# Source indices of a graph kernel loaded once and copied into the gather slots by VectorE, in place of one DMA per tile

## The reference

```python
h = relu(layernorm(x));  z = h @ W                       # layer 1: attention, 8 heads of 16
e = leaky_relu(el[src] + er[dst]);  a = exp(e - max)     # el, er: z times attn_l, attn_r per head
x = x + segment_sum(z[src] * a, dst) / segment_sum(a, dst) + bias
h = relu(layernorm(x));  s, v = h @ W_up                 # layer 2: messages
w = silu(silu(edge_f @ A1 + b1) @ A2 + b2) @ A3
x = x + segment_sum(products of s[src], v[src], edge_y and w, dst) / 10 @ W_out
```

## Time and profile before

| | |
|---|---|
| median of 3 runs | 4219.83 us (4218.35 to 4221.5) |
| profiled execution: span, first to last instruction | 5708.3 us |
| busy in it: TensorE matmul / weight load | 3872.9 / 2962.4 us |
| busy in it: GpSimd / VectorE / ScalarE | 3121.2 / 1850.8 / 547.9 us |
| DMA | 239.77 MB, 42 GB/s on average |

### The profile page before, as it was taken

One profiled execution on the slowest core, in us unless ns is written; L12 is line 12 of the kernel. 1 busy time (PEld: TensorE's weight loads), 2 busy tenths in 40 slices (PEclk: granted clock), 3 DMA queues, 4 the chain that ended last, 5 costly groups with the idle time before them and its releaser, 6 DMA issues.

```text
span 5708.3 us, 68375 instructions
## 1 busy us (share of the span) xinstructions
PE 3872.9 (68%) x18070; PEld 2962.4 (52%) x18071; DVE 1850.8 (32%) x4774; ACT 547.9 (10%) x1093; POOL 3121.2 (55%) x3153
## 2 busy tenths in 40 slices
PE   3566666766666666666657776776777776667767
PEld 2455555555555555555545555555555555555545
DVE  6122222222222222222234443433333434333334
ACT  1000000000000000000021111111111111111111
POOL 4555555555555555555535555555555555555554
PEclk8555555555555555555567777777777877777777
DMA  3111111111111111111111111111111111111111
GB/s 75 40 40 40 40 40 41 41 42 40 41 40 41 40 41 39 41 40 40 40 43 41 42 45 41 44 45 41 42 43 43 44 44 41 44 40 43 42 41 34
DMA packets 259081, 239.77 MB, mean 42 GB/s; under 512 B 179890, under 2 KB 205596, under 8 KB 259068
## 3 DMA queue, kind: packets, MB, share of 16 engines
q0 software_dynamic: 100352, 212.14, 15.2%
q1 hardware_dynamic: 158572, 26.68, 2.6%
q10 hardware_dynamic: 144, 0.80, 0.0%
HBM read 229.11 MB, written 10.23 MB: 42 GB/s over the span
## 4 chain that ended last, share of the span: by engine, by line
another core or an unknown queue 43%; PE 22%; issue 17%; DVE 11%; DVEq 4%; ACT 2%; DMA 0%; ACTq 0%; SPq 0%
PE pair L1085 5%; PE pair L1050 5%; DVE share L809 4%; PE pair L1044 3%; PE pair L1083 3%; PE pair L1040 2%; DVEq L768 2%; ACT share L502 1%; PE pair L1062 1%; PE pair L1004 1%; PE pair L987 1%; DVE share L743 1%; DVE share L800 1%; DVE share L799 1%
## 5 line engine op out<-in xcount | busy, mean ns | idle before, releaser
L401 POOL DMA_INDIRECT rows<-z_tab,idx x1568 | 1531.6, 977 | 1290.3 <-DVEq L813 748.9
L401 POOL DMA_INDIRECT rows<-up_tab,idx x1568 | 1549.4, 988 | 1208.6 <-DVEq L896 718.1
L1004 PE MATMUL pair<-share 128*128 128x48 f32 x3136 | 1000.7, 416 | 122.6 <-issue 122.3
L1004 PEld LDWEIGHTS pair<-share 128*128 128x128 f32 x3136 | 808.4, 317 | 279.4 <-issue 273.3
L1085 PE MATMUL pair<-share 128*128 128x144 f32 x3136 | 859.4, 359 | 129.8 <-issue 129.3
L1083 PEld LDWEIGHTS pair<-share 128*128 128x128 f32 x3136 | 587.2, 219 | 443.2 <-issue 342.9
L1050 PE MATMUL pair<-a_bd,share 128*128 128x256 f32 x1576 | 465.9, 448 | 394.1 <-ACT share L504 371.1
L877 DVE TENSOR_TENSOR share<-share,y_sb 128x768 f32<-128x768 f32 x392 | 375.6, 958 | 977.1 <-remote 662.1
L1083 PE MATMUL pair<-share 128*128 128x48 f32 x3136 | 585.7, 269 | 140.0 <-issue 121.2
L1085 PEld LDWEIGHTS pair<-share 128*128 128x128 f32 x3136 | 561.3, 221 | 128.6 <-issue 128.0
L987 PE MATMUL pair<-er_win,share 96*128 96x32 f32 x1576 | 377.2, 404 | 333.0 <-issue 268.4
(11 more groups left out here) (138 smaller groups left out, 2085.3 us busy)
## 6 DMA issues: line engine op xcount, KB each, us to landing
rows<-z_tab,idx POOLq DMA_INDIRECT x1568
rows<-up_tab,idx POOLq DMA_INDIRECT x1568
idx<-in_src SPq DMA_DIRECT2D x396, 4.0 KB
er_win<-er_tab SPq DMA_DIRECT2D x396, 3.0 KB
ef_sb<-in_edge_f SPq DMA_DIRECT2D x198, 32.0 KB
z_tab<-rows SPq DMA_DIRECT2D x7, 476.0 KB, 3.1
y_sb<-in_edge_y SPq DMA_DIRECT2D x198, 16.0 KB
x_sb<-in_x SPq DMA_DIRECT2D x7, 448.0 KB, 6.9
```

What stands on the lines that cost most here:

```text
L401: pool.indirect_dma_start(out=rows[:, s, t, 0:width], out_offset=None, in_=table, in_offset=bass.IndirectOffsetOnAxis(ap=indices[:, t:t + ...
L1004: t.matmul(bank[2 + h][:, 0:WIN], msg[:, h, i, :], hot[:, s, i, :], start=(i == 0), stop=(i == T - 1))
```

## The change

A tile idx_all holds the source indices of all 200 tiles (196 and the first four again). One DMA on ScalarE's queue fills it at the start; for that the array is laid out with the partition first. Each loop's index DMA on SP, its semaphores and the `landed` count are gone. VectorE instead copies 128x8 indices from idx_all into the gathers' slot, at the place where the slot's old indices are known to be used: after L804 in the attention stage, and behind the wait for the rows in the message stage. Four such copies fill the slots before the first gather, ahead of L709. GpSimd waits for the count of copies, `idx_set`.

```diff
+        idx_all = sb("idx_all", [P, NG + U, T], I32)
...
-            for s in range(U):
-                sp.dma_start(idx[:, s, :], src[s, :, :]).then_inc(s_idx[s], 16)
             store_rows(s_in, ZW, z_tab)
-
-            def load_idx(s, group):
-                sp.dma_start(idx[:, s, :], src[bass.ds(group, 1), :, :].rearrange("a p t -> (a p) t"))\
-                  .then_inc(s_idx[s], 16)
...
                     load((s + AHEAD) % U, q * U + (s + AHEAD))
-                    hold(sp, s_l["landed"], i + 1)
-                    load_idx(s, q * U + (s + U))
...
-                            hold(pool, s_idx[s], (n + before) * 16 + 16)
+                            hold(pool, idx_set, (n + before) * U + (s + 1))
                             hold(pool, s_l["rows_free"], n * U + (s + 1))
...
             act.dma_start(dst_i, dst).then_inc(loads["dst"], 16)
+            act.dma_start(idx_all[:, :, :], src).then_inc(loads["src"], 16)
...
+            dve.wait_ge(loads["src"], 16)
+
+            def set_idx(s, group):
+                v.tensor_copy(idx[:, s, :], idx_all[:, bass.ds(group, 1), :].rearrange("p a t -> p (a t)"))\
+                    .then_inc(idx_set, 1)
+
+            for s in range(U):
+                set_idx(s, s)
...
                         dve.wait_ge(s_l1["rows"][s], q * (16 * T) + 16 * T)
-                        dve.sem_inc(s_l1["landed"], 1)
...
                         v.tensor_scalar(e3[3], e3[2], 0.0, None, ALU.min).then_inc(s_l1["score"], 1)
+                        set_idx(s, q * U + (s + U))
                         one_hot((s + 1) % U, q * U + (s + 1))
...
                                 dve.wait_ge(s_l2["rows"][s], q * (16 * T) + 16 * T)
-                                dve.sem_inc(s_l2["landed"], 1)
+                                set_idx(s, q * U + (s + U))
```

More of the change, by code:

```diff
@@ L177, in gnn_kernel @@
         loads = {n: sem(f"load_{n}") for n in
-                 ("x0", "x1", "const", "dst", "w", "attn", "bias", "mlp", "up", "out_w", "win")}
+                 ("x0", "x1", "const", "dst", "src", "w", "attn", "bias", "mlp", "up", "out_w", "win")}
         zeroed = sem("zeroed")
@@ L197, in edge_sems @@
         def edge_sems(tag, names):
-            return named(tag, ("rows_free", "added", "open", "landed") + names) \
+            return named(tag, ("rows_free", "added", "open") + names) \
                 | {n: sems(f"{tag}_{n}_slot", U) for n in ("rows", "in")}
-        s_idx = sems("idx", U)
+        idx_set = sem("idx_set")
         s_l1 = edge_sems("l1", ("hot", "turned", "hot_turned", "er", "score", "exp", "msg", "agg"))
@@ L312, in _ @@
                     sp.wait_ge(s_max["free"], g + 1)
-                    sp.dma_start(idx_max[:, :], src[bass.ds(g, 1), :, :].rearrange("a p t -> (a p) t"))\
-                      .then_inc(s_max["idx"], 16)
                     sp.dma_start(dst_row.rearrange("a (t p) -> a t p", t=T),
@@ L414, in _ @@
                 with pool.Fori(0, NG) as g:
-                    hold(pool, s_max["idx"], (g + 1) * 16)
+                    hold(pool, s_max["idx"], g + 1)
                     gather(0, idx_max, z_tab, ZW, s_max["rows"])
@@ L685, in _ @@
                 with dve.Fori(0, NG) as g:
+                    v.tensor_copy(idx_max[:, :], idx_all[:, bass.ds(g, 1), :].rearrange("p a t -> p (a t)"))\
+                        .then_inc(s_max["idx"], 1)
                     dve.wait_ge(s_max["turned"], g + 1)
@@ L1112 @@
         "x": np.concatenate([np.asarray(x), np.zeros((NB * P - NODES, HIDDEN), np.float32)]),
-        "src": np.concatenate([np.asarray(src), np.zeros(extra, np.int32), np.asarray(src)[:U * GE]])
-            .reshape(NG + U, P, T),
+        "src": np.ascontiguousarray(
+            np.concatenate([np.asarray(src), np.zeros(extra, np.int32), np.asarray(src)[:U * GE]])
+            .reshape(NG + U, P, T).transpose(1, 0, 2)),
         "dst": np.ascontiguousarray(
```

## The result

The changed kernel takes 4259.96 us (median of 4 runs, 4252.17 to 4261.8), the kernel before 4219.09 us (4217.27 to 4221.5): a ratio of 1.0093, 95% interval 1.0079 to 1.0107, 41 us slower. The forecast was slower, 4245 us.

A forecast was written before the change was run, and what follows sets the result against it. GpSimd's nearly unbroken stream of gathers was taken as the bound. 25 us of longer holds plus 0.5 us at the start, on the 4219.8 us median, gave 4245 us; range 4160 to 4280 us.

The forecast's parts named there:

- The bound: Both edge stages: undisturbed, GpSimd issues gathers almost without a break, 9.98 us per group of eight.
- The subtraction of 1467 us of slot waits: Profile span 5708.3 us less GpSimd's waits at L813 and L896 leaves 4241.3 us, 0.5% above the median.
- The floor: 392 groups of gathers, 3914 us, plus 228.6 us around them: 4142 us, leaving about 77 us for anything else.
- 160 groups have one: Lower count of groups with a held gather, from 77 us at 0.48 us a hold; costs 16 us.
- The index loads leave SP: Loop index DMAs gone from SP: cost and gain 0, bound 1.8 us.
- The opening: Four copies ahead of the first gather delay L714 and the gather it holds: 0.5 us, at most 0.7.
- The copy's length is hidden: 392 copies, 67 us of VectorE's time, called free beside GpSimd; rival with that length on the path: 4287 us, chance 0.09.
- The shift of 0.10 us: Copies move VectorE's two-input operations 0.10 to 0.17 us later in both stages; each held gather costs 0.10 us more.
- the 25 of the sum: Cost in us of held gathers lengthened by the shift, taken between 16 and 39 us.
- The phase: Where operations fall against gathers, from first groups: second L809 holds in the attention stage, L877 in the message stage.
- The rival of a hold that falls away: Attention stage: the gather's moment slides ahead of the second L809; up to 77 us faster, about 4175 us, chance 0.29.
- That L804 holds nothing, and so the copy: One-input L804 held no gather, so the copy itself costs 0; bound 0.17 us a group, 67 us.

The follow-up runs named there:

- e8: Kernel before plus eight unread 128x8 copies per attention-stage group, after the scores; 5732.22 us, ratio 1.0035, where the kernel before takes 5700 us.
- e12: Changed kernel with copies last, attention-stage inputs from PSUM and message-stage product in four operations; 6132.66 us, ratio 1.0671, where the kernel before takes 5700 us.
- e3: Changed kernel with each loop copy moved behind the group's last two-input operation on VectorE; 4210.1 us, ratio 0.9966.
- e4: Changed kernel with the loop's index copies on ScalarE in place of VectorE; 4215.12 us, ratio 0.9985.
- e1: Kernel before, unchanged, traced without the long pauses; 4222.2 us, ratio 1.0003.
- e6: Changed kernel, copies in place, attention stage's long operations reading one input from PSUM so none has two in SBUF; 4194.82 us, ratio 0.9936.
- e2: Kernel before with all its index DMAs, plus one unread 128x8 copy per group at the change's two places; 4242.75 us, ratio 1.0047.
- e9: Kernel before plus one unread 128x512 copy per attention-stage group, after the scores; 5685.01 us, ratio 0.995, where the kernel before takes 5700 us.
- e11: Eight unread 128x8 copies per attention-stage group of the kernel before, run once more; 5778.15 us, ratio 1.0058, beside 5748.13 us for the kernel before.

## Why the prediction was right, and where it was off

*The bound.* Right: an undisturbed run is a stream of gathers. The subtraction of 1467 us of slot waits was sound. Its reason was not: I put the pauses down to the profiled execution as such, and on the chips of e8 to e12 the kernel takes 5700 us in unprofiled runs too.

*The floor.* A term that was mis-sized. I took 95.9 us between the stages and 41.2 behind from the paused trace, where they are 65.6 and 21.0. So the floor is 4092 us and the lengthening 124 us, not 77. "160 groups have one" should have been 543 held gathers (over 960 ns: 197 and 346).

*The index loads leave SP: "cost and gain 0".* Nearly. Nothing waited for them, but without the `landed` count VectorE starts the scores 0.05 us sooner. e3 is 12 us faster than before, e4 7 us: again by place.

*The opening.* I had 0.5 us; the first gather starts at 91.6 us as before (91.8 in e1), and the hold behind it is 5.81 us in both. 0.

*The copy's length is hidden.* Right, by e3, e4 and e6.

*The shift of 0.10 us.* This is the term of the sum that was off most. Medians after the eighth gather: the one-hot operation of the attention stage moved from 3.59 to 3.67 us (0.08: the copy's 0.14 less the 0.06 of the dropped count), the second L877 of the message stage from 4.40 to 4.60, 0.20. Half of that isn't the copy's length. From the landing of the rows to the first product are 0.13 us in e1, 0.21 in e2 and 0.30 in the changed kernel (medians). The product starts 0.08 us after the copy in both, so 0.09 of the 0.17 do overlap. In e2 the shifts are 0.09 and 0.10, near the 0.10 forecast, and the lengthening grows by 26.7 us, close to the 25 of the sum. So the price of 0.10 us was right, and the sum came out as 14.5 + 27.2 = 41.7 us because the message stage had twice the shift.

*The phase.* Taken from the first groups, it named the second L809 as the holder. In the steady stream L743 holds most of the attention stage's gathers. The first group did not even show the forecast: the gathers at the opening moved with the held one, so that the moment stayed 0.16 us into the second product, and the hold 0.53 us. The rival of a hold that falls away did happen in some groups, as in the one shown, and was paid back by the products. Its condition was misread: a hold falls away at once when the moment comes under some 0.16 us into the operation, and not only ahead of it. That the attention stage as a whole lost and didn't gain was not worked out beforehand, and the forecast has luck in it there.

*That L804 holds nothing, and so the copy.* Right in its result for 128x8, wrong as a rule: e9's copy of 0.42 us holds. The row of L804 was misread. The moment at 112.87 is 0.14 us into it, where nothing was seen to hold, and L804's 0.24 us there, against a median of 0.195, is the conflict seen from the other side. The Trainium skill ("GPSIMD Engine Reference", Key points) has contention with VectorE instructions in a 2-port perf mode or with two SBUF inputs. On two inputs the traces agree: 0.26 and 0.42 us by L743 and L811. The long copy's 0.26 us fits the other half, but no trace here shows in which mode an instruction ran.

## What to carry to other kernels

When one engine issues a steady stream and is the bound, look at the spread of its instructions against their median before anything else: here that spread was all that VectorE's work could change. A short operation on an engine with time to spare can cost something or nothing, by what it moves behind it (41 us, or none behind the long operations); put it after them. And before using a trace's stage lengths as a floor, compare its span with the runs' time: if it is longer, every stage in it may be.

## What the runs showed of the hardware

- A gather (indirect DMA issued by GpSimd) has one moment, 0.13 us after its start, at which VectorE can hold it. Then it is held to the end of the operation: 0.26, 0.42, 5.8 us. Operations with one input in SBUF and one in PSUM don't do it: with those, the attention stage's lengthening fell from 75.1 to 8.8 us (changed kernel and e6).
- An operation with both inputs in SBUF held no gather whose moment was less than 0.14 us into it. At a moment 0.15 or 0.16 us in, the gather could go free and the operation was the longer one: L745 0.61 for 0.56 us, the 128x8 copy 0.23 for 0.17.
- A one-input copy of 128x512 held a gather 0.26 us; 13 gathers with a 128x8 copy over their moment took 944 to 948 ns, and that copy is over at 0.17 us.
- Two two-input operations back to back can hold a gather through both: 1.11 us, at a moment 0.19 us into the first (e11), and so for 165 of the 190 gathers of e8 and e11 with a moment there. In the other traces a moment in the first let go at its end. What decides between the two wasn't found.
- The same kernel took 4220 us on some chips and 5700 us on others. The gathers' median is 944 ns on both the earlier trace rows; what differs is that VectorE frees its slots late, among stretches in which TensorE, VectorE and ScalarE stand idle together. The cause of the pauses isn't in the traces.
